# A graph network's gathering passes: branch-free batches, twelve buffers instead of six, packed window bounds

## What is computed

```python
# L2: both directions of every edge
agg_fwd = segment_sum(w[:, None] * x[col], row, num_segments=n)
agg_bwd = segment_sum(w[:, None] * x[row], col, num_segments=n)
out = 0.5 * (agg_fwd @ W_src.T + b_src) + 0.5 * (agg_bwd @ W_dst.T + b_dst)
# L3: weighted mean over the edges of a target
msg = edge_attr[:, None] * node[src]
ssum = segment_sum(msg, dst, num_segments=n)
agg = ssum / maximum(cnt, 1.0)[:, None]
h = agg @ W_rel.T + b_rel + node @ W_root.T
```

## Time and profile before

| | |
|---|---|
| median of 3 runs | 9336.75 us (9331.7 to 9336.76) |
| the profiled execution, its own time | 9342.07 us |
| its span in the profile | 9340.4 us |
| PE, PEld busy | 7261.6 us (78%), 5838.2 us (63%) |
| DVE, ACT, POOL busy | 6413.4 us (69%), 3252.4 us (35%), 4037.3 us (43%) |
| mean DMA rate | 135 GB/s |
| mean granted clock of PE | 0.881 |
| produce_p | about 4900 to 5388 us |
| gathering pass of L2f | 5389 to 6194 us |
| produce_q of L2b, its loop | 6253 to 6892 us |
| gathering pass of L2b | 6896 to 7573 us |
| produce_q of L3, its loop | 7788 to 8428 us |
| gathering pass of L3 | 8432 to 9140 us |

### The profile page before, as it was taken

The page is one execution under the profiler, slowest core; times in us unless marked ns, Lnnn a source line. Parts: engine busy times, 40 slices in busy tenths (PEclk is TensorE's granted clock), DMA queues, the critical chain, the costliest instruction groups (busy, mean ns, idle before and its releaser), DMA issues. The chain is left out here.

```text
span 9340.4 us, 229910 instructions
## 1 busy us (share of the span) xinstructions
PE 7261.6 (78%) x60542; PEld 5838.2 (63%) x60851; DVE 6413.4 (69%) x20871; ACT 3252.4 (35%) x9379; POOL 4037.3 (43%) x4385
## 2 busy tenths in 40 slices
PE   4855677899968888888868977758877775886777
PEld 4855566544446666666667766646666664666665
DVE  5999888511167777777777766656666676666667
ACT  3533322222223333333235500025520025557882
POOL 2000577000057777777625567730037740006771
PEclk7975789999977777777789999989999988999997
DMA  0000466300024444444347866665556644556663
GB/s 21 2 2 1 110 140 140 91 24 24 23 73 105 107 105 106 106 105 105 91 147 271 289 183 191 191 156 230 230 199 191 192 156 178 230 230 183 184 182 106
DMA packets 645062, 1262.07 MB, mean 135 GB/s; under 512 B 126526, under 2 KB 183433, under 8 KB 644569
## 3 DMA queue, kind: packets, MB, share of 16 engines
q1 hardware_dynamic: 424337, 704.50, 23.0%
q0 software_dynamic: 199040, 544.46, 21.7%
q10 hardware_dynamic: 21452, 10.20, 0.4%
HBM read 780.96 MB, written 477.75 MB: 135 GB/s over the span
## 5 line engine op out<-in xcount | busy, mean ns | idle before, releaser
L1063 PE MATMUL PS<-w,GS 128*128 128x128 f32 x12176 | 1641.7, 284 | 499.9 <-DVE AREA L1008 224.2
L1063 PEld LDWEIGHTS PS<-w,GS 128*128 128x128 f32 x12176 | 1459.6, 192 | 682.3 <-DVE w L967 437.6
L1188 POOL DMA_INDIRECT GS<-xbuf,KI x964 | 1031.2, 1070 | 1759.7 <-ACTq L132 710.1
L1171 POOL DMA_INDIRECT GS<-t1d,KI x1564 | 1493.6, 955 | 488.0 <-issue 459.6
L2395 DVE TENSOR_SCALAR AREA<-PS,IP 128x512 bf16<-128x512 f32 x1116 | 837.7, 751 | 439.6 <-PE PS L2405 361.1
L967 DVE TENSOR_TENSOR w<-IO,KI 128x512 f32<-128x512 f32 (+1 forms) x1355 | 808.6, 597 | 424.6 <-issue 413.4
L2419 PE MATMUL PS<-AREA 128*128 x13392 | 961.1, 220 | 11.1 <-ACT GS L2373 1.4
L2419 PEld LDWEIGHTS PS<-AREA 128*128 128x128 bf16 x13392 | 843.8, 98 | 170.2 <-issue 49.2
L2373 ACT ACTIVATE GS<-PS 128x512 f32<-128x512 f32 x1116 | 666.3, 597 | 613.8 <-PE PS L2419 613.5
L1188 POOL DMA_INDIRECT GS<-pbuf,XR x558 | 595.3, 1067 | 209.4 <-issue 101.4
L1598 ACT ACTIVATE w<-PS,w 128x48 f32<-128x48 f32 x1564 | 341.7, 301 | 926.9 <-PE PS L1593 926.9
(11 more groups left out here) (410 smaller groups left out, 12508.2 us busy)
## 6 DMA issues: line engine op xcount, KB each, us to landing
xbuf<-GS SPq DMA_DIRECT2D x1116, 256.0 KB
XR<-in_edge_attr SPq DMA_DIRECT2D x780, 256.0 KB
pbuf<-AREA SPq DMA_DIRECT2D x482, 256.0 KB
GS<-t1d,KI POOLq DMA_INDIRECT x1564
GS<-xbuf,KI POOLq DMA_INDIRECT x964
GS<-pbuf,XR POOLq DMA_INDIRECT x558
AREA<-t2d ACTq DMA_DIRECT2D x121, 64.0 KB
keyd<-AREA POOLq DMA_INDIRECT x482
```

What stands on the lines that cost most here:

```text
L1063: i = e.matmul(PS[:, s % 3, 0:128], feats(s)[0:m, r, 0:D], SELW[s % 3][0:m, width * r:width * r + 128], start=(r == 0), stop=(r == 3))
L1171: e.indirect_dma_start(GS[0:m, s, r, 0:wide], None, table, bass.IndirectOffsetOnAxis(ap=idx[0:m, c:c + 1].bitcast(U32), axis=0)).then_inc( ...
L1188: e.indirect_dma_start(GF[:, 512 * s:512 * s + 512], None, buf, bass.IndirectOffsetOnAxis(ap=idx[:, b:b + 1].bitcast(U32), axis=0)).then_i ...
```

## The change

Five parts. (1) `sum_pass` takes the place of `edge_pass` in the three gathering passes. Its fast form has no branch per batch: in Q order a batch always lies in one window, and in P order the fast form adds at the chunk's first node and is right where no chunk spans more than 128 nodes; a flag `FLP`, computed once in `p_bases`, chooses between it and a general form in the P passes. `bd` is counted by the matmuls themselves, and the one-element memset goes, as do the clearing of the comparison tiles and two first matmuls. PE reads no bounds any more. (2) Twelve buffers (`gslot`): six in `GS`, six in `R`. (3) DVE loads bounds once per twelve batches: in Q order four numbers that each pack three windows of 7 bits, in P order three. (4) `produce_q` loads its offsets once per 18 batches, six numbers of three packed windows each; a register per place in the turn is masked, multiplied and shifted in an inner loop of three turns. The first and the last two turns load as before. (5) `p_bases` computes the packed numbers and the flag.

```diff
-    RNG = sb("RNG", [128, max(2 * NR, 8 * NCK, 2 * NBQ) + 2], I32)
+    RNG = sb("RNG", [128, max(2 * NR, 9 * NCK, 2 * NBQ) + 2], I32)
+    FLP = sb("FLP", [1, 1], I32)
+    NQ3 = (NITQ - 2) // 3
...
+            v = IOX[96:97, UN:UN + 3 * UN * NQ3].rearrange("o (q j s) -> o q j s", j=3, s=UN)
+            t = PK[96:97, 0:UN * NQ3].rearrange("o (q s) -> o q s", s=UN)
+            link(e.scalar_tensor_tensor(out=t, in0=v[:, :, 2], scalar=128.0, in1=v[:, :, 1], op0=ALU.mult, op1=ALU.add))
+            link(e.scalar_tensor_tensor(out=t, in0=t, scalar=128.0, in1=v[:, :, 0], op0=ALU.mult, op1=ALU.add))
+            link(e.tensor_copy(RNG[96:97, NBQ:NBQ + UN * NQ3], PK[96:97, 0:UN * NQ3]))
...
+            e.tensor_copy(RNG[96:97, NBQ + UN * NQ3:NBQ + UN * NQ3 + NBQ // 3], t)
...
+            v = RNG[32:33, 0:8 * n].rearrange("o (c t) -> o c t", t=8)
+            e.tensor_copy(RNG[32:33, 8 * n:9 * n], v[:, :, 0])
+            link(e.tensor_tensor(DR[0][32:33, :], v[:, :, 1], v[:, :, 0], ALU.subtract))
+            link(e.tensor_reduce(FLP[0:1, 0:1], DR[0][32:33, :], AX, ALU.max))
...
+    GRING = 12
+
+    def gslot(s):
+
+        return GF[:, 512 * s:512 * s + 512] if s < 6 else R[:, 512 * (s - 6):512 * (s - 5)]
+
     def gather_groups(p, bd, buf, idx, nb):
 
-        ready = [p.sem(f"g{s}") for s in range(UN)]
+        ready = [p.sem(f"g{s}") for s in range(GRING)]
 
         @p.on("gpsimd")
         def _(e):
             for b in range(nb):
-                s = b % UN
-                if b >= UN:
-                    e.wait_ge(bd, b - UN + 3)
-                e.indirect_dma_start(GF[:, 512 * s:512 * s + 512], None, buf,
+                s = b % GRING
+                if b >= GRING:
+                    e.wait_ge(bd, b - GRING + 3)
+                e.indirect_dma_start(gslot(s), None, buf,
                                      bass.IndirectOffsetOnAxis(ap=idx[:, b:b + 1].bitcast(U32), axis=0)
                                      ).then_inc(ready[s], 16)
-            for s in range(UN):
-                e.wait_ge(ready[s], 16 * ((nb - 1 - s) // UN + 1))
+            for s in range(min(GRING, nb)):
+                e.wait_ge(ready[s], 16 * ((nb - 1 - s) // GRING + 1))
...
-            held = {}
-
-            def step(b, s, it):
-                if s == 0:
-                    held[0] = ranges(e, 3, it * UN, UN, 384 * 97)
+
+            def step(b, s, it, w_):
                 if s + 2 < UN:
                     spread(b + 2, s + 2, it)
                 elif not (isinstance(it, int) and it == NITQ - 1):
@@ -2417,11 +2423,30 @@
                 for r in range(4):
                     for k in range(3):
                         i = e.matmul(PS[:, 3 + s % 3, 128 * r:128 * r + 128], OHT[s % 3][:, 128 * r:128 * r + 128],
-                                     TAB[:, bass.ds(held[0][s] + 128 * k, 128)], start=(k == 0), stop=(k == 2))
+                                     TAB[:, bass.ds(w_ + 128 * k, 128)], start=(k == 0), stop=(k == 2))
                 i.then_inc(gm, 1)
+
+            def alone(it):
+                v = ranges(e, 3, it * UN, UN, 384 * 97)
+                for s in range(UN):
+                    step(it * UN + s, s, it, v[s])
             spread(0, 0, 0)
             spread(1, 1, 0)
-            peeled(e, NBQ, UN, step)
+            alone(0)
+
+            wr = [reg(e, "wr") for _ in range(UN)]
+            with e.Fori(0, NQ3) as o:
+                v = ranges(e, 3, o * UN + NBQ, UN, 128 ** 3 - 1)
+                for s in range(UN):
+                    e.reg_mov(wr[s], v[s])
+                with e.Fori(0, 3) as j:
+                    for s in range(UN):
+                        it = o * 3 + j + 1
+                        w_ = e.snap(((e.snap(wr[s], min_val=0, max_val=128 ** 3 - 1) & 127) * 384).with_bounds(max_val=384 * 97))
+                        e.reg_alu(wr[s], wr[s], 7, ALU.arith_shift_right)
+                        step(it * UN + s, s, it, w_)
+            for it in range(1 + 3 * NQ3, NITQ):
+                alone(it)
...
+    def turns(e, nb, un, f):
+
+        n = nb // un
+        for b in range(un):
+            f(b, b, 0)
+        if n > 2:
+            with e.Fori(1, n - 1) as it:
+                for s in range(un):
+                    f(it * un + s, s, it)
+        for b in range(un * max(1, n - 1), nb):
+            f(b, b % un, b // un)
+
+    def sum_pass(p, nb, inq, keys, ready, ACC, weight=None):
+
+
+        acc, oh, dv, bd, kx, mm = (p.sem(k) for k in ("acc", "oh", "dv", "bd", "kx", "mm"))
+        wd = p.sem("wd") if weight is not None else None
+        SEL = [p.tile([128, 4, 128]) for _ in range(3)]
+        KX, TY, TZ = p.tile([128, 4]), p.tile([1, 1]), p.tile([1, 1])
+
+        def feats(s):
+            return gslot(s).rearrange("p (r f) -> p r f", r=4)
+
+        def sel(e, q, kl):
+            return e.tensor_tensor(SEL[q][:], IO[:].unsqueeze(1).to_broadcast([128, 4, 128]),
+                                   kl.unsqueeze(2).to_broadcast([128, 4, 128]), ALU.is_equal)
+
+        def wide(e):
+            return nc.values_load_multi_w_load_instructions(
+                FLP[0:1, 0:1], engines=[e.engine], min_val=0, max_val=NN + 1,
+                skip_runtime_bounds_check_because="a difference of node numbers")[1][0]
+
+        def fast_vector(e):
+
+            e.nop().then_inc(bd, 2)
+            w1, w2 = reg(e, "w1"), reg(e, "w2")
+            low = {}
+
+            def lows(s, it):
+                if s == 0:
+                    m = min(GRING, nb - GRING * it) if isinstance(it, int) else GRING
+                    if inq:
+                        low["v"] = ranges(e, 3, it * 4 + (NBQ + UN * NQ3), (m + 2) // 3, 128 ** 3 - 1)
+                    else:
+                        low["v"] = ranges(e, 1, it * 3 + 8 * NCK, (m + 3) // 4)
+                if inq:
+                    v = low["v"][s // 3]
+                    low[s] = (((v >> 7 * (s % 3) if s % 3 else v) & 127) * 128).with_bounds(max_val=128 * (NW - 1))
+                else:
+                    low[s] = low["v"][s // 4]
+
+            def add(b, q, w_):
+                e.wait_ge(bd, b + 3)
+                past(e, acc, b, 1)
+                e.tensor_tensor(ACC[:, bass.ds(w_, 128)], ACC[:, bass.ds(w_, 128)], PS[:, q, 0:128], ALU.add
+                                ).then_inc(acc, 1)
+
+            def step(b, s, it):
+                sel(e, s % 3, keys[:, bass.ds(b * 4, 4)]).then_inc(oh, 1)
+                if s >= 2:
+                    add(b - 2, (s - 2) % 3, low[s - 2])
+                elif not isinstance(b, int) or b >= 2:
+                    add(b - 2, (s + 1) % 3, e.snap((w1, w2)[s], min_val=0, max_val=NN + 1))
+                lows(s, it)
+                if s == GRING - 1:
+                    e.reg_mov(w1, low[s - 1])
+                    e.reg_mov(w2, low[s])
+            turns(e, nb, GRING, step)
+            for b in (nb - 2, nb - 1):
+                s = b % GRING
+                last = s if b // GRING == (nb - 1) // GRING else None
+                add(b, b % 3, low[s] if last is not None else e.snap((w1, w2)[s - GRING + 2], min_val=0, max_val=NN + 1))
+
+        def fast_tensor(e):
+            def step(b, s, it):
+                if weight is None:
+                    e.wait_ge(ready[s], it * 16 + 16)
+                else:
+                    e.wait_ge(wd, b + 1)
+                e.wait_ge(oh, b + 1)
+                past(e, acc, b, 3)
+                for r in range(4):
+                    i = e.matmul(PS[:, s % 3, 0:128], feats(s)[:, r, :], SEL[s % 3][:, r, :], start=(r == 0), stop=(r == 3))
+                i.then_inc(bd, 1)
+            turns(e, nb, GRING, step)
...
+        @p.on("vector")
+        def _(e):
+            e.memset(ACC, 0.0).then_inc(dv, 1)
+            e.wait_ge(dv, 1)
+            if inq:
+                fast_vector(e)
+            else:
+                fl = wide(e)
+                with e.If(fl <= 128):
+                    fast_vector(e)
+                with e.Else():
...
+        @p.on("tensor")
+        def _(e):
+            if inq:
+                fast_tensor(e)
+            else:
+                fl = wide(e)
+                with e.If(fl <= 128):
+                    fast_tensor(e)
+                with e.Else():
...
+        sum_pass(p, nb, inq, keys, ready, ACC, weight)
         p.run()
 
     def p_l2f():
         produce_p(t2d)
-        aggregate(pbuf, GP, NBQ, 2, KQ, AB[:, 0, :])
+        aggregate(pbuf, GP, NBQ, True, KQ, AB[:, 0, :])
 
     def p_l2b():
         produce_q(t3d)
-        aggregate(xbuf, GQ, NBP, 1, KP, AB[:, 1, :])
+        aggregate(xbuf, GQ, NBP, False, KP, AB[:, 1, :])
```

115 lines of the change are left out of this document (77 added, 38 removed).

## The result

| kernel | median, us | runs | ratio to the kernel before, 95% interval |
|---|---|---|---|
| before | 9334.53 | 4 | |
| the change | 9453.99 (9443.21 to 9467.88) | 4 | 1.0129 (1.0111 to 1.0147) |

A forecast was written before the change was run, and what follows sets the result against it. POOL's gathers were taken to bound L2f and L2b, with buffer waits added in L3, and PE's instruction stream produce_q. The terms -40.7 - 21 - 17 - 50 - 2 - 15 + 4 gave -142, so 9195 us, range 9095 to 9310.

The forecast's parts named there:

- produce_q: Both produce_q stages: two of three loads saved against added register instructions, -15 us, bounds -130 to +60.
- the addition is hidden at most in part: produce_q: added register instructions, 1.2 us per turn, partly hidden because some 0.5 us of full-queue waiting goes.
- The 1.57 us: produce_q: time lost at each turn's head to the load of bounds; two turns of three lose their load.
- registers hidden nowhere: produce_q: the term's upper bound, every added register instruction costing its full time, +60 us.
- The starts: Starts of L2f, L2b, L3: twelve buffers let the thirteenth gather start after about 15 us, saving 40.7 us.
- The steady steps of L2f and L2b: Gather steps in L2f and L2b fall to 1.33 us, saving 21 and 17 us.
- two thirds of the present stretch: L2f and L2b: share of the present lengthening of gathers taken to remain, giving a step of 1.33 us.
- stretches as before: Rival for the three passes: step 1.37 us everywhere, L3's waits gone, 9254 us; chance 0.20.
- the slow rival: Rival: comparisons fall on POOL's gather starts, step 1.482 us, 9412 us; decides from 1.44; chance 0.06.
- L3: L3's steady part: waits for buffers go with twelve buffers, step falls to 1.325 us, saving 50 us.
- L2f's last 72 batches: End of L2f: no gain, since neither buffers nor branches touch these batches; bounds 0 and 5 us either way.
- p_bases: p_bases and flag: eight more dependent DVE instructions, +4 us; the flag surely picks the fast pass.

The follow-up runs named there:

- Run 10: Changed kernel with old produce_q loop, bounds eight apart, comparison row in PSUM, plus three register instructions per produce_q batch: 10786.38 us on the slow chip, 0.9997.
- run 4: Changed kernel with the comparison's row of 128 numbers read from PSUM instead of SBUF in the three passes: 9291.02 us, 0.9942.
- run 11: Changed kernel with gathers held back as if there were six buffers: 10794.56 us, 1.0005 on the slow chip; repeated on another, 9488.58 us, 1.0151.
- the four executions with the changed passes: The change's profiled execution, Run 1, a near repeat of it (9304.54 us), and the change measured again beside run 11 (9467.78 us).
- run 6: Kernel before with two repairs only, produce_q's bounds eight numbers apart and the comparison's row of the passes in PSUM: 9126.60 us, 0.9770.
- Run 1: Changed kernel with the loop of produce_q as it was before, six bounds loaded per turn without packing: 9282.24 us, 0.9928.
- run 12: Changed kernel with comparison row in PSUM and produce_q loading twelve plain bounds per two turns: 10448.19 us, 0.9682 on the slow chip; 8976.52 us, 0.9603 on a usual one.
- run 2: Changed kernel with produce_q's packed bounds stored eight numbers apart instead of six: 9402.59 us, 1.0061.
- run 7: Changed kernel with comparison row in PSUM and produce_q loading 18 plain bounds at once, three turns written out: 9052.31 us, 0.9688.
- runs 3: Changed kernel with the old loop of produce_q and its bounds stored eight numbers apart: 9181.77 us, 0.9818.
- runs 9: Changed kernel with old produce_q loop, bounds eight apart, comparison row in PSUM, plus register additions compiled to one a turn: 10529.33 us on the slow chip, 0.9756.

## Why the prediction was wrong

**produce_q, the failed step** (-15 forecast, +154 measured by the cut at the last matmul, outside its own bounds of -130 to +60). The prediction took three things from the earlier trace rows and had two wrong. First, "each batch gets two more register instructions on PE": there are three, since a move of the packed value stands beside the shift and the mask; the order of the instructions doesn't show it, the sequencer's rows do. Second, and the larger one: "the addition is hidden at most in part", with 0.5 us per turn that "is waiting for a full queue, which goes". By its terms a turn without a load takes 5.3 + 1.2 - 0.5 = 6.0 us; it takes 6.91. I charged the registers 1.2 us a turn against an unchanged batch of 0.88, and let two loads of three pay for it. Run 10 shows that three instructions a batch move the batch itself, from 0.886 to 1.03 and more: the old stream, at 0.74 us a batch, hid part of the load and branch behind the array, and with three more instructions that cover is gone in every turn. They cost 1.39 us a turn there, where the sum had 0.7 net. A turn without a load became as long as a turn with one had been, and the load that was left stood open, in 3.2 to 4.0 us instead of 1.75 to 2.6. The 1.57 us, too, were not the load's alone: in the trace of before the stream spends 0.49 us at a turn's end on the loop's own count and branch before the load begins (6514.81 to 6515.30), and the changed inner loop keeps a branch in every turn. What would have told it beforehand is the sequencer's cadence over one batch, read from the trace of before, set against 0.886: 0.74 + 3 x 0.1 is over it. The upper bound, "registers hidden nowhere", still left the two saved loads in the sum at their full visible 1.57 us, so it was not an upper bound, and by its own terms (-0.3 + 1.5 = 1.2 a round, 60 rounds) it is +72, not +60.

Third, the alternation of 7.3 and 6.4 us between turns wasn't asked about. The range of the load row, "0.84 to 2.09", was taken as scatter and averaged; it was for the most part the places of the bounds.

**The starts: right.** -13.7, -12.3 and -13.1 measured for -14.4, -12.9 and -13.4. But only 25 of these 39 us are the buffers'; with six buffers the thirteenth gather of the changed pass comes sooner than that of the old one by itself.

**The steady steps of L2f and L2b: the stretch read rightly, its change forecast with the wrong sign.** What stretches the gathers is shown by run 4. But "two thirds of the present stretch" was not to be had: the mean gather went from 1.07 to 1.08 and 1.10 us. Of the rivals, "stretches as before" (1.37) is nearest in L2f, and L2b stands halfway between it and the threshold of the slow rival (1.44). Long gathers (over 1.0 us) are 44% in L2f and 50% in L2b, where they were one in three: a comparison tied to the matmuls doesn't keep clear of POOL's starts. In L2f it depends on how long DVE stands at the turn's head: with the load of bounds at 0.97 us the step is 1.375 to 1.389 in four runs with twelve buffers, with 0.35 us 1.336 and 1.340. Why L2b is above L3 wasn't tried.

**L3: the size nearly right in this execution, -55 for -64, by a partly wrong cause.** Its waits went, as forecast, but not by twelve buffers, as run 11 shows. In the four executions with the changed passes L3 gains 38 to 56 us, so that the size is part luck.

**L2f's last 72 batches: right.** Their gathers start 1.46 us apart instead of 1.62, which looks like 12 us gained. But their matmuls stand 1.65 us apart in both kernels, and the transfers run at 157 GB/s before and 159 after. POOL only runs further ahead of them, and the wait comes behind the last gather: 11 us of what the table books on produce_q's first stretch.

**p_bases: consistent**, +4.4 for +4, and the flag chose the fast pass. But L2f's first gather starts at 5388.4 to 5394.6 us in the four executions named above and run 4, and at 5389.4 and 5384.2 in the kernel before and run 6, so one pair can't confirm 4 us. The last stretch's +7 was in no term.

Without produce_q the sum would have been -127 forecast against some -47 measured in the two profiled executions: still a gain, well under half of what was forecast. Run 1 is that kernel: 0.9928, 65 us by its medians.

## What to carry to other kernels

Before adding register instructions to a loop, compare the sequencer's time per batch with the array's. Three more a batch took it from 0.74 to 1.03 us, past the array's 0.886; they cost 1.39 us a turn of six, since the batches took the stream's time and what had been hidden behind the queue (a load, a branch) came out as well. What they would cost below the array's time no run here tells. Loading more values at once was right up to twelve (72 us, run 12), and 18 gained nothing; packing them to do so was not. When a deeper ring of buffers makes an issuing engine finish sooner, measure at the last consumer and not at the last issue. Look at the spread of a load's durations for a pattern before averaging it: where the values lie in their row changed the time of the same load by up to threefold. And where an engine's long instructions slow another's, change the operand that they share (here one row moved to PSUM, 160 us) rather than when they meet.

## What the runs showed of the hardware that was not expected

- A load of bounds into registers takes 0.35 us for four numbers whose index is a multiple of 4 and 0.97 where it leaves 2 (DVE, L2f); for six numbers on PE 1.1 and 2.0 by the same rule, and 0.85 from a multiple of 4 in run 10. Twelve from a multiple of 4 take 1.15, no more than six, and 18 take 2.11. Three numbers, whose index runs through all remainders in L2b, take 0.75 throughout.
- PE's clock fell to 1.2 GHz behind most of the loads over which the spreads stood 2.8 to 4.0 us apart (23 and 24 of 31 in the two stages of the change, 20 of 30 in each of run 2, 21 and 19 of 30 in run 7), and behind none where they stood 1.7 to 2.8 apart (turns of before, runs 3, 10 and 12). In the change, the matmuls behind such a gap (PE's timeline):

```profile
6624.64 0.38 PE L2414 MATMUL PS<-AREA,ONB 128*128 128x512 bf16 x1
6624.88 0.98 PE L2425 MATMUL PS<-AREA 128*128 x12
6628.57 0.61 PE L2414 MATMUL PS<-AREA,ONB 128*128 128x512 bf16 x1 [2.71 <-issue]
6629.00 1.50 PE L2425 MATMUL PS<-AREA 128*128 x12
6630.29 0.63 PE L2414 MATMUL PS<-AREA,ONB 128*128 128x512 bf16 x1
```

The same twelve matmuls take 1.50 us instead of 0.98 for some three batches (window view, 6628 to 6630 us: granted clock 0.50). In the changed loop this costs less than it seems: in run 2 three turns take 22.9 us with a fall and 22.5 without, since the stream runs ahead meanwhile and the next batches then go at the array's 0.89. In run 7, where the array is the bound, a fall costs 1.7 us.
- One chip took 10787 us for the kernel before, 15% more than the others. In runs 9, 10 and 12 there the gathers took the same 956 ns, but steps of 1.50 to 1.55 us, waiting for transfers; a turn of produce_q took the same time as elsewhere (5.98 us in run 12, on both chips).
